# A graph network of four layers on one core: longer lags in layer two's node pass, another order in its edge pass, loops of eight steps written out

## What is computed

```python
x = _layernorm(x + L0(x))   # messages times edge rows, summed by node, two matmuls, batch norm
x = _layernorm(x + L1(x))   # mean of edge rows, 512 hidden units
x = _layernorm(x + L2(x))   # attention over edges, 8 heads, ELU
x = _layernorm(x + L3(x))   # attention over edges and self loops, 4 heads, ELU

# L2, for each edge (src, dst)
ft = (feat @ W).reshape(n, 8, 32)
e = leaky_relu(a1[src] + a2[dst]);  m = segment_max(e, dst)
ex = exp(e - m[dst]);  alpha = ex / segment_sum(ex, dst)[dst]
out = elu(segment_sum(ft[src] * alpha, dst))
```

## Time and profile before

| | |
|---|---|
| median of 3 runs | 5583.04 us (5579.09 to 5586.88) |
| the profiled execution | 5618.38 us, span 5616.6 us |
| busy, share of the span | PE 80%, POOL 67%, DVE 60%, ACT 34% |
| mean granted TensorE clock | 0.897 |
| layer two's edge pass | about 3246 to 3891 us of the span |
| layer two's node pass | about 3891 to 4581 us |
| last pass | about 4965 to 5617 us |

### The profile page before, as it was taken

How to read it: one execution, slowest core, us unless ns; L and a number is a source line. 1 busy time by engine, 2 the same in 40 slices (tenths; PEclk the granted TensorE clock), 3 DMA queues, 4 the chain that set the end, 5 groups by cost and what they waited for, 6 DMA issues and landing times. The chain is left out here.

```text
span 5616.6 us, 68003 instructions
## 1 busy us (share of the span) xinstructions
PE 4466.3 (80%) x17208; PEld 2963.8 (53%) x17208; DVE 3371.4 (60%) x9357; ACT 1907.7 (34%) x3319; POOL 3767.0 (67%) x3395
## 2 busy tenths in 40 slices
PE   2477669999999999999999967774777656656765
PEld 1255435556666666666666656664666533322222
DVE  1255456566666666666666547676555548945655
ACT  0011135532222222222222244453444420026765
POOL 7488644445777777777777767774555568856674
PEclk7688889999999999999999988886888978878887
DMA  9999899987744334433334255655777756658886
GB/s 378 307 202 207 193 279 365 361 310 275 260 136 133 128 127 132 134 132 127 123 131 132 99 181 200 217 212 176 259 264 261 264 189 226 240 172 282 309 310 218
DMA packets 530526, 1214.70 MB, mean 216 GB/s; under 512 B 172297, under 2 KB 267697, under 8 KB 530370
## 3 DMA queue, kind: packets, MB, share of 16 engines
q1 hardware_dynamic: 344392, 963.16, 48.4%
q0 software_dynamic: 147728, 214.04, 14.3%
q10 hardware_dynamic: 38250, 35.85, 2.0%
HBM read 623.69 MB, written 721.15 MB: 239 GB/s over the span
## 5 line engine op out<-in xcount | busy, mean ns | idle before, releaser
L1123 PE MATMUL psum<-W2b,arena 128*128 128x256 f32 x3136 | 725.2, 379 | 0.0
L840 DVE TENSOR_SCALAR arena<-arena 128x256 f32<-128x256 f32 x784 | 476.9, 669 | 388.2 <-POOL arena L835 383.4
L1104 PE MATMUL psum<-arena,W1b 128*128 128x512 f32 x1568 | 699.1, 599 | 0.0
L1123 PEld LDWEIGHTS psum<-W2b,arena 128*128 128x128 f32 x3136 | 573.1, 190 | 66.3 <-issue 0.5
L1946 POOL DMA_INDIRECT hd_d<-arena,FL x392 | 382.2, 975 | 306.6 <-DVE arena L1992 185.2
L618 PE MATMUL psum<-arena,half 128*128 128x324 f32 x980 | 355.2, 528 | 284.0 <-ACT arena L409 156.6
L2092 POOL DMA_INDIRECT arena<-fin_d,FL x392 | 427.3, 1090 | 184.6 <-issue 118.0
L1012 ACT ACTIVATE arena<-psum,hbias 128x512 f32<-128x512 f32 x392 | 270.0, 689 | 804.2 <-PE psum L1104 794.7
L1104 PEld LDWEIGHTS psum<-arena,W1b 128*128 128x128 f32 x1568 | 289.8, 190 | 402.4 <-issue 402.4
L967 POOL DMA_INDIRECT xl_d<-arena,FL x392 | 389.0, 992 | 118.7 <-issue 116.4
L959 POOL DMA_INDIRECT xd_d<-arena,FL x360 | 378.6, 1052 | 99.5 <-issue 99.2
(11 more groups left out here) (291 smaller groups left out, 8926.4 us busy)
## 6 DMA issues: line engine op xcount, KB each, us to landing
arena<-in_x SPq DMA_DIRECT2D x194, 512.0 KB
x_d<-arena SPq DMA_DIRECT2D x194, 512.0 KB
tab<-zero SPq DMA_DIRECT2D x11, 5832.0 KB
arena<-x_d SPq DMA_DIRECT2D x105, 512.0 KB
h_d<-arena SPq DMA_DIRECT2D x97, 528.0 KB
arena<-h_d SPq DMA_DIRECT2D x97, 528.0 KB
h_d<-arena SPq DMA_DIRECT2D x98, 512.0 KB
arena<-h_d SPq DMA_DIRECT2D x98, 512.0 KB
```

The costliest lines, as they stand in the source:

```text
L840: v.tensor_scalar(y[:, j, :], r[:, j, :], self.mv[:, j, 0:1], self.rs[:, j:j + 1], ALU.subtract, ALU.mult).then_inc(self.s["y"], 1)
L1104: last = pe.matmul(psum[:, HB[c], :], W1b[:, f, c * P:(c + 1) * P], x1T[:, f, :], start=False, stop=(f == FH - 1))
L1123: last = pe.matmul(outB(j), hid[:, c, j * P:(j + 1) * P], W2b[:, c, :], start=(c == 0), stop=(c == KH - 1))
```

## The change

In the edge pass the transposed blocks get four banks and four tiles (NT = 4) and the products four banks, PE transposes three columns ahead instead of one, ACT copies two ahead; the ELU stands at column 4 of a group; DVE's order in iteration g becomes logits(g), finish(g-2), shares(g), chain(g) whole; LAG is 23; the last finish is put into the middle of the joining code. In the node pass the projected rows' store counts in `gd`, apart from the normalised rows' store, `to_rows` runs six steps behind instead of four (HLAG = 6), the projected rows are stored four steps behind instead of two, and the transposed tiles are four. All loops of node pass and last pass are written out.

```diff
-            F0, NF = 2, 6
+            NT, NF = 4, 4
-            LAG = 25
+            LAG = 23
...
-                tr(0)
+                for c in range(NT - 1):
+                    tr(c)
                 for c in range(C):
-                    if c + 1 < C:
-                        tr(c + 1)
+                    if c + NT - 1 < C:
+                        tr(c + NT - 1)
                     mm(c)
...
-                    wait(act, r["mm"], c - 1)
-                    act.activation(xT[:, c % 2, :, :], psum[:, c % 2, :].rearrange("p (i n) -> p i n", n=P), ACT.Copy).then_inc(r["ev"], 1)
+                    wait(act, r["mm"], c - NT + 1)
+                    act.activation(xT[:, c % NT, :, :], psum[:, c % NT, :].rearrange("p (i n) -> p i n", n=P), ACT.Copy).then_inc(r["ev"], 1)
...
-                    elif j == 5 and g >= 2:
+                    elif j == 4 and g >= 2:
                         elu(g - 2)
...
-                logits(0)
-                shares(0)
                 for g in range(NE):
-                    if g + 1 < NE:
-                        logits(g + 1)
-                    chain(g, 0, 3)
-                    if g > 0:
-                        finish(g - 1)
-                    if g + 1 < NE:
-                        shares(g + 1)
-                    chain(g, 3, JE)
+                    logits(g)
+                    if g > 1:
+                        finish(g - 2)
+                    shares(g)
+                    chain(g, 0, JE)
...
-                finish(NE - 1)
-                join.vector(v)
+                finish(NE - 2)
+                join.vector(v, lambda: finish(NE - 1))
...
-            xT = take([2, FH, STEP])
+            xT = take([NB, FH, STEP])
             hs = take([NB, J, HW])
+            HLAG = 6
...
-                wait(eng, n_w[b], 32 * k.turn(NB) + W4[b])
+                wait(eng, n_w[b], 16 * k.turn(NB) + W4[b])
+
+            def heads_out(eng, k):
+
+                b = k.slot(NB)
+                wait(eng, gd[b], 16 * k.turn(NB) + 16 * (NE // 2))
...
-                    if not (k.known() and k.s < 2):
-                        store_h(k.plus(-2))
-                run_beats(sp, NS, body, NH, peel=NH, tail=NH)
+                    if not (k.known() and k.s < HLAG - 2):
+                        store_h(k.plus(2 - HLAG))
+                for s in range(NS):
+                    body(beat(s, NH))
...
-                    if not (k.known() and k.s < 4):
-                        to_rows(k.plus(-4))
-                run_beats(v, NS, body, NH, peel=NH)
+                    if not (k.known() and k.s < HLAG):
+                        to_rows(k.plus(-HLAG))
+                for s in range(NS):
+                    body(beat(s, NH))
...
-                run_beats(act, NS, body, NH)
+                for s in range(NS):
+                    body(beat(s, NH))
```

More of the change, by code:

```diff
@@ L1164, in gnn_program @@
         W4 = [W2[b] + 16 * THIRDS[b] for b in range(NB)]
-        W5 = [W4[b] + 32 * USES[b] for b in range(NB)]
+        W5 = [W4[b] + 16 * USES[b] for b in range(NB)]
         W6 = [W5[b] + 16 * THIRDS[b] for b in range(NB)]
@@ L1233, in vector @@
                 v.tensor_copy(newrow, self.endrow).then_inc(r["fr"], 1)
+                if meanwhile:
+                    meanwhile()
                 n0 = 9 * (T - 1)
@@ L1269, in edge_pass2 @@
             xl = take([2, JE, D])
-            xT = take([2, 4, P])
+            xT = take([NT, 4, P])
             ft = take([2, JE, TW])
@@ L1439, in g_scalar @@
                 act.wait_ge(r["zero"], 5)
-                ev(0)
+                for c in range(NT - 2):
+                    ev(c)
                 for c in range(C):
-                    if c + 1 < C:
-                        ev(c + 1)
+                    if c + NT - 2 < C:
+                        ev(c + NT - 2)
                     projected(c)
@@ L1898, in body @@
                         for f in range(FH):
-                            last = pe.matmul(psum[:, 2 + j, 0:HW], xT[:, k.slot(2), f, j * P:(j + 1) * P], Wg[3][:, f, :], start=(f == 0), stop=(f == FH - 1))
+                            last = pe.matmul(psum[:, 2 + j, 0:HW], xT[:, k.slot(NB), f, j * P:(j + 1) * P], Wg[3][:, f, :], start=(f == 0), stop=(f == FH - 1))
                         if j % 2 == 1:
@@ L1922, in evac @@
                     act.wait_ge(r["tr"], k.s + 1)
-                    wait(act, r["mm"], 2 * (k.s - 1))
+                    wait(act, r["mm"], 2 * (k.s - NB + 1))
                     for f in range(FH):
-                        act.activation(xT[:, k.slot(2), f, :], psum[:, f, :], ACT.Copy).then_inc(r["xT"], 1)
+                        act.activation(xT[:, k.slot(NB), f, :], psum[:, f, :], ACT.Copy).then_inc(r["xT"], 1)
                 def body(k):
@@ L2030, in last_pass @@
             n_g = gs + sc
-            H0 = [16 * USES[b] + 16 * EIGHTHS[NB + b] for b in range(NB)] + [16 * (NE // 2) * n for n in (2, 2, 1, 1)]
+            H0 = [16 * USES[b] + 16 * EIGHTHS[NB + b] for b in range(NB)] + [16 * (NE // 2) * n + 16 * USES[b] for b, n in enumerate((2, 2, 1, 1))]
             X0 = [16 * USES[b] + 16 * EIGHTHS[b] for b in range(NB)]
@@ L2079, in body @@
                         store(k.plus(-NB))
-                run_beats(sp, NS, body, NH, tail=NH)
+                for s in range(NS):
+                    body(beat(s, NH))
                 for s in range(NS - NB, NS):
@@ L2109, in body @@
                     last.then_inc(r["r"], 1)
-                run_beats(pe, NS, body, NH)
+                for s in range(NS):
+                    body(beat(s, NH))
             def l_scalar(act):
@@ L2197, in body @@
                         halved(k.plus(-2))
-                run_beats(v, NS, body, NH)
+                for s in range(NS):
+                    body(beat(s, NH))
                 stats(beat(NS - 1, NH))
```

31 lines of the change are left out of this document (16 added, 15 removed).

## The result

The changed kernel takes 5646.39 us (median of 4 runs, 5641.7 to 5659.92), the one before 5584.96 us beside it (4 runs, 5579.09 to 5592.69): ratio 1.0113, 95% interval 1.0091 to 1.0135, 61 us slower. The prediction had 5541.

A forecast was written before the change was run, and what follows sets the result against it. No engine was full; the order of waits between engines was taken as the bound. Edge pass 38 us gained, node pass 4, written-out loops and last pass 0: 5583 - 42 = 5541 us, range 5505 to 5618.

The forecast's parts named there:

- The term for its longer instructions: Edge pass: GpSimd's instructions lengthen as more of them meet large two-input VectorE instructions, about 7 us added.
- (a): Edge pass: the 3 to 4 us in which the ring of gathers fills at the start stay.
- (c): Edge pass: some of GpSimd's waits for other engines stay, taken as 8 us, a seventh.
- (d): Edge pass: the two scatters that LAG moves forward cost nothing.
- Rival D: No effect: GpSimd's instructions stretch as waits go; edge pass gains 10 us, node pass loses 0 to 10; 5573 to 5590; chance 0.08.
- The new circle: Node pass: root, `to_rows`, product, transposes, product, transposes, copies, guess, root; 12.9 us per two steps at full clock.
- The clock: Node pass: TensorE's clock falls after 3.8 us of idling in one piece; 0.6 us a pair added, giving 13.5.
- The late release: Node pass: TensorE's release came 1.4 us after its modelled end, unexplained; not priced in the sum.
- rival B: Node pass: TensorE's release late in the new circle too, delaying `to_rows`; net 13 to 41 us slower, 5596 to 5624; chance 0.27.
- E: Node pass: half clock after idling in every pair, 14.5 us; 42 us lost against 38 gained, 5587; chance 0.05.
- the old circle: Node pass before: root, normalising, copies, transposes, product, `to_rows`, statistics, next root; 13.7 us per two steps.
- C: Node pass: no clock loss, part of the lateness gone, 12.9 us a pair or less; 32 us more gained; 5490 to 5515; chance 0.15.

The follow-up runs named there:

- e6: Kernel before with only the edge pass's change: edge pass two 616.6 us, ratio 0.9955.
- e13: e7 plus 7 matmuls into an unused bank in front of each odd step's product: node pass 630.8 us, pair 12.33, ratio 0.9858.
- e7: Changed kernel without the node pass's 392 scatters and the waits for them: node pass 719.9 us, pair 14.25, ratio 1.0011.
- e1: Changed kernel with the node pass's lag back at 4: node pass 689.4 us, ratio 0.9929.
- e4: Kernel before with the steps of node pass and last pass written out, nothing else: node pass 689.1 us, ratio 0.9982.
- e2: Changed kernel with lag 5 in the node pass: node pass 663.0 us, ratio 0.9887.
- e5: Changed kernel, lag 6, with TensorE transposing two steps ahead instead of one: node pass 654.5 us, ratio 0.9888.
- e12: e7 with SyncE storing the heads a second time as straight rows: node pass 719.1 us, ratio 0.9985.
- e8: Changed kernel plus 8 matmuls into an unused bank in front of each odd step's product: node pass 803.4 us, ratio 1.0153.
- e15: e5 plus 3 matmuls into an unused bank in front of every step's product: node pass 667.6 us, ratio 0.9931.

## Why the prediction was wrong

**Edge pass: right, the size 10 us too large.** GpSimd became the bound, by the named cuts. Forecast 38, measured 28.2 in the profile and 25 by e6. The term for its longer instructions (7) measured 7.9. The waits that stay (3.6 + 8) measured 16.9. Of these 10.9 lie in the start, where (a) had 3.6, and none for TensorE later, where (c) had 8. The other 6.0 are the first scatter's wait: LAG brings it two columns forward and the new order brings the first `finish` later, and (d) had said that this costs nothing. The estimate for the end, no wait for the last `finish`, held. Four microseconds more of issue were not in the sum.

The reading of the earlier trace rows, that a part of the 2.02 us is lost and not all, needs its times. The scatter starts 1.05 us into L1539 and ends 0.88 us behind it, and alone it would take 0.97: nearly all of the overlap is lost. Rival D still didn't occur, because nearly as many of GpSimd's transfers overlapped a VectorE instruction longer than 1.5 us before (128) as after (134).

**Node pass: the mechanism right, the sum wrong, and this made the sign.** Forecast -4 us, measured +84.3. The new circle runs as drawn. Its price at full clock was 0.6 too high, 12.9 against 12.33 in e13, which hid a part of what the other terms lacked. Two terms failed and made the sign.
- *The clock*, "I add 0.6, less than half of the 1.55 ... because the phase's mean is 0.91". It measured 1.92 a pair. The mean of 0.91 was that of the old order; the new one puts most of the idle time in one piece ahead of one product. The rows were misread besides. In the old order the transposes come first behind the idle time and the product after them; from 4008.00 to 4012.40 the granted clock was 0.86, so only the beginning of the product of 4.40 us was at half clock. In the new order the product comes first: it averages 5.47 us, and the transposes behind it run at full clock, 1.06. So the full 1.55 us would have been nearer to 1.92, but not for the reason given.
- *The late release*, put at nothing in the sum and given to rival B: 0.88 a pair (e7), from scatters of GpSimd that stand beside the circle, not in it.
- *The base* was sound: 13.7 from one pair against a mean of 13.57, within 1%.

12.33 + 1.92 + 0.88 = 15.13; the parts are the differences between e13, e7 and after, so they must add up, and another order of taking things away might share them out otherwise; against 13.57 it is 1.56 a pair, 75 us over 48 intervals, and about 9 us lie at the ends, 5 forecast.

**The rivals.** B and E were each half true, and they add. B named the slower side and the late release, but put it at `to_rows`; it fell on the copies behind the second transposes. E had the place and the cause of the clock. Each was priced alone, E at 5587, B at 5596 to 5624. My case against B, that the old circle could not turn in 13.7 us with late releases, did not bear on the new one. B's upper figure, 15.3 us a pair with 0.6 for the clock, lies near the measured 15.13, but by luck: its full-clock circle was 0.6 too dear, its late release 0.9 too dear and its clock 1.3 too cheap. The measured 5646 passes the range's upper end by 28 us; no rival had both prices whole. C and D didn't occur.

**Loops, semaphores, tiles**: 0 forecast; e1 and e4 show the node pass unchanged within 2 us. Writing out brings 10 us in all in e4, the upper bound, and its interval reaches nearly to no change. **Last pass**: "equal within 10 us" failed, 29.8 us shorter in the profiles, but not by the change's own lines alone (e6). Because of it "the profiled one was 35 us above the median, and I take that as equal" was a weak step as well: the passes' differences sum to +23 in the profiles, and the medians differ by 61.

**The better kernel.** e2 and e5 are 1.1% faster than the one before: the edge pass's new order, and lag 5, or lag 6 with transposes two ahead.

## What to carry to other kernels

A longer lag cuts one circle and may close another through an engine that works in order: walk from the instruction that waits to what is queued behind it, and back to the waiting one, before the lag is chosen. Here neither the lag nor the number of steps transposed ahead decided, but their difference: 3 closed one circle, 5 the other, 4 neither. If the walk closes, price the burst behind its idle time at half clock, from a row whose granted clock has been looked up, and the releases as late as the trace shows them anywhere. When a lag is raised, move what stands behind the waiting instruction ahead of it, by as many steps as leave slack on both sides.

## What was not expected of the hardware

- ScalarE's copies start 0.04 us behind the recorded end of TensorE's transposes in all pairs of e7, e12 and e13. Beside GpSimd's scatters they started about 2.1 us behind it in every second pair. With matmuls added behind the transposes, they started when those had ended, 3.6 to 3.8 us behind, in 26 of 48 pairs (e8). The 392 scatters of the node pass cost it 54.6 us, though nothing in the circle waits for them by name and there is DMA bandwidth to spare (e12). The way in which they do it is open.
- Adding TensorE work took 89 us off a pass where the scatters were left out (e13). With the scatters the same means made it longer (e8 by 29 us, e15 by 13).
